# Unread TensorE products, earlier table loads and an earlier second round of routing in the drain of a decoder layer

## The reference, cut to what matters

```python
x = _layernorm(x + attention(x, W_K, W_Q, W_V, W_O))        # causal, 16 heads of 128
x = _layernorm(x + cross_attention(x, ctx_2048, ...))       # 16 heads of 16, 256 image keys
# mixture of experts: E = 8, K = 2, F = 1024
gate_probs = softmax(x @ gate_w + gate_b)
weights, selected = top_k(gate_probs, 2); weights = weights / sum(weights)
h = gelu(einsum('nd,edf->enf', x, w1) + b1)
expert_out = einsum('enf,efd->end', h, w2) + b2
x = _layernorm(x + einsum('ne,end->nd', comb, expert_out))
```

## Time and profile before

| | us |
|---|---|
| median of 3 runs | 613.43 (612.69 to 613.81) |
| the profiled execution, its own time | 612.67 |
| its span | 610.2 |
| PE busy | 548.7 (90%) |
| DVE busy | 366.8 (60%) |
| ACT busy | 309.3 (51%) |
| POOL busy | 169.2 (28%) |

### The profile page before, as it was taken

How to read it: one execution, slowest core, us unless ns; L and a number is a source line. 1 busy time by engine, 2 the same in 40 slices (tenths; PEclk the granted TensorE clock), 3 DMA queues, 4 the chain that set the end, 5 groups by cost and what they waited for, 6 DMA issues and landing times.

```text
span 610.2 us, 12615 instructions
## 1 busy us (share of the span) xinstructions
PE 548.7 (90%) x3875; PEld 478.2 (78%) x3875; DVE 366.8 (60%) x1150; ACT 309.3 (51%) x837; POOL 169.2 (28%) x280
## 2 busy tenths in 40 slices
PE   2899999999999999999987989998769999999930
PEld 2689989898998989899876756655469999999930
DVE  6075565656556565655668657776377456665645
ACT  1365454545545454554554668755553545544523
POOL 5131311213121121301452888041620010000253
PEclk9999999999999999999989789979769999999985
DMA  8740040404104040380000000010211544444124
GB/s 273 254 186 24 31 161 26 180 17 153 54 24 165 22 184 0 138 347 14 1 2 1 1 2 4 2 71 10 87 53 53 179 166 180 173 181 165 61 78 128
DMA packets 18403, 58.75 MB, mean 96 GB/s; under 512 B 3168, under 2 KB 7520, under 8 KB 13760
## 3 DMA queue, kind: packets, MB, share of 16 engines
q1 hardware_dynamic: 14048, 38.00, 17.2%
q10 hardware_dynamic: 1728, 12.58, 5.6%
q0 software_dynamic: 2592, 7.74, 3.6%
HBM read 35.83 MB, written 22.41 MB: 95 GB/s over the span
## 4 chain that ended last, share of the span: by engine, by line
PE 81%; DVE 8%; issue 3%; ACT 2%; DMA 2%; POOL 2%; DVEq 1%; ACTq 0%; POOLq 0%
PE bank L605 13%; PE bank L607 12%; PE bank L606 12%; PE bank L932 8%; PE bank L662 5%; PE bank L644 4%; PE bank L819 4%; PE bank L652 4%; PE bank L835 3%; PE bank L762 2%; PE bank L663 2%; PE bank L643 2%; DVE w_lo L1536 2%; PE bank L869 1%; PE bank L690 1%
## 5 line engine op out<-in xcount | busy, mean ns | idle before, releaser
L1228 ACT ACTIVATE hT<-bank,b 128x128 f32<-128x128 f32 x152 | 53.6, 367 | 63.2 <-PE bank L932 60.1
L932 PE MATMUL bank<-xgT,w 128*128 128x128 f32 x608 | 73.9, 281 | 0.8 <-ACT hT L1228 0.8
L932 PEld LDWEIGHTS bank<-xgT,w 128*128 128x128 f32 x608 | 72.2, 197 | 1.0 <-ACT hT L1228 1.0
L605 PE MATMUL bank<-xT_hi,wqk_hi 128*128 128x512 f32 x128 | 56.8, 444 | 11.0 <-DVE wqk_lo L1283 11.0
L1037 ACT ACTIVATE Pr<-Sm,nmax 128x128 f32<-128x128 f32 x64 | 25.8, 403 | 71.1 <-DVE nmax L1292 71.0
L1292 DVE CUSTOM_DVE_ANT_0 Sm<-bank,mask 128x128 f32<-128x128 f32 (+1 forms) x128 | 40.9, 356 | 34.4 <-PE bank L644 34.3
L1422 DVE TENSOR_REDUCE xnmax<-bank 128x2 f32<-128x512 f32 x64 | 43.7, 687 | 27.3 <-PE bank L798 26.6
L606 PE MATMUL bank<-xT_lo,wqk_hi 128*128 128x512 f32 x128 | 51.1, 399 | 0.0
L607 PE MATMUL bank<-xT_hi,wqk_lo 128*128 128x512 f32 x128 | 51.0, 399 | 0.0
L1128 ACT ACTIVATE xPT<-bank 128x512 f32<-128x512 f32 x64 | 37.7, 597 | 26.2 <-PE bank L819 26.0
L605 PE MATMUL bank<-w_hi,hT_hi 128*128 128x256 f32 x152 | 44.7, 294 | 2.8 <-DVE hT_lo L1549 2.8
(11 more groups left out here) (232 smaller groups left out, 1516.7 us busy)
## 6 DMA issues: line engine op xcount, KB each, us to landing
w<-in_w ACTq DMA_DIRECT2D x12, 1024.0 KB, 6.5
w_raw<-in_w_attn SPq DMA_DIRECT2D x32, 256.0 KB, 3.6
x_slots<-w SPq DMA_DIRECT2D x8, 1024.0 KB, 5.5
y_slots<-w SPq DMA_DIRECT2D x7, 1024.0 KB, 7.4
w<-in_w SPq DMA_DIRECT2D x4, 1024.0 KB, 7.9
y_slots<-ys POOLq DMA_DIRECT2D x19, 128.0 KB, 2.0
xg<-x_slots SPq DMA_DIRECT2D x18, 128.0 KB, 2.1
xT_raw<-in_xT SPq DMA_DIRECT2D x2, 512.0 KB, 5.5
```

Of the source, the lines that this page charges most:

```text
L605: mm(out, lh, rh, start=start, stop=False)
L932: last = mm(ps_h[f % 4][:, 0:P], w1[e % 2][:, c, f * P:(f + 1) * P], xgT[:, c, :], start=c == 0, stop=c == DC - 1)
L1228: A(hT[:, f, :], ps_h[f % 4][:, 0:P], ACT.Gelu_apprx_tanh, bias=b1[:, e, f:f + 1])\
```

## The change

On PE a helper `keep_warm(n, out)` is new: n bf16 products of ones by ones, 128x512, into a bank that is not read before it is started anew. Calls of it stand at six places of the drain: 4 before the third row transposes (`x2t_unit(2)`, in step 69), 3 before the last `z_back` (step 78), 1 before the last output products, 10 before the last row transposes, 2 before the last gate products, 2 behind the transposes of the first static tile. `ffn_tile` is cut in two, `h_products` and `y_products`, and the first three of eight h blocks of the first static tile stand ahead of the last `rank_unit`. Round one moves up: its gate products from step 71 to 70 and ahead of `x_pv`, its ranks from 74 to 72, ACT's evacuation from 70 to 69, DVE's part from 72 and 75 to 71 and 73. On ACT the Sqrt table is loaded behind the last exponential of the items and the Gelu table behind `gate_exp`. On DVE `xgt_evac(2)` stands ahead of the search for the indices, `count_tiles` and `gate_weights` move into the loop over the static tiles, `gate_weights` to the second.

```diff
             def ffn_tile(e, i):
+                h_products(e, i, 0, FC)
+                y_products(e, i)
+            def keep_warm(n, out):
+                for _ in range(n):
+                    mm(out[:, :], ones_bf[:, :], ones_bf[:, :].unsqueeze(1).to_broadcast([P, 4, P]), start=True, stop=True)
...
+                if i == STEPS_X - 3:
+                    keep_warm(3, ps_xt[1])
                 if j >= 13 and (j - 13) % ZUNIT == 0 and j - 13 < ITEMS:
                     z_back((j - 13) // ZUNIT)
+                if i in (61, 70):
+                    gate_unit((61, 70).index(i))
...
+                if i == 69:
+                    pe.wait_ge(s["xmax_ready"], ITEMS)
+                    keep_warm(4, ps_gate)
                 if i in (55, 59, 69):
                     x2t_unit((55, 59, 69).index(i))
-                if i in (61, 71):
-                    gate_unit((61, 71).index(i))
-                if i in (64, 74):
-                    rank_unit((64, 74).index(i))
+                if i in (64, 72):
+                    rank_unit((64, 72).index(i))
+            keep_warm(1, ps_xt[1])
             xo_unit(TT - 2)
             xo_unit(TT - 1)
+            keep_warm(10, ps_xt[1])
             x2t_unit(TT // 2 - 1)
+            keep_warm(2, ps_xt[1])
             gate_unit(2)
             xg_transposes(0)
+            keep_warm(2, ps_xt[1])
+            h_products(0, 0, 0, 3)
             rank_unit(2)
-            for e in range(EARLY):
+            h_products(0, 0, 3, FC)
+            y_products(0, 0)
+            for e in range(1, EARLY):
                 ffn_tile(e, e)
... ACT
-                if i in (56, 60, 70):
-                    x2t_evac((56, 60, 70).index(i))
+                if i in (56, 60, 69):
+                    x2t_evac((56, 60, 69).index(i))
+                if i == ITEMS + LAG:
+                    A(warm[:, :], eps_rms[:, :], ACT.Sqrt)
...
             gate_exp()
+            A(warm[:, :], eps_rms[:, :], ACT.Gelu_apprx_tanh)
... DVE
-                if i == 72:
+                if i == 71:
                     gate_logits(1)
                     gate_index(1)
                     gate_select(1)
-                if i == 75:
+                if i == 73:
                     slots(1)
...
             gate_shift()
+            xgt_evac(2)
             gate_index(2)
             gate_select(2)
-            xgt_evac(2)
             slots(2)
-            count_tiles()
-            gate_weights()
             dve.wait_ge(s["b2_in"], 16)
             for e in range(EARLY):
+                if e == 0:
+                    count_tiles()
                 h_splits(e)
                 xgt_evac(e + 3)
                 if e == 0:
                     w2_low(1)
                 else:
+                    gate_weights()
                     slot_weights()
                 y_add(e, e)
```

More of the change, by code:

```diff
@@ L923, in xg_transposes, with h_products @@
                 last.then_inc(s["xgt_done"], 1)
[L925 to L929, removed]
+            def h_products(e, i, a, z):
+                if a == 0:
+                    pe.wait_ge(s[f"w_in{e % 2}"], 32 * (e // 2 + 1))
+                    pe.wait_ge(s["xgt_ready"], i + 1)
+                for f in range(a, z):
                     pe.wait_ge(s["h_gelu"], i * FC + f + FC - 3)
@@ L934, in ffn_tile, with y_products @@
                     last.then_inc(s["h_done"], 1)
+            def y_products(e, i):
                 xg_transposes(i + 1)
@@ L943, in ffn_tile @@
                 last.then_inc(s["y_done"], 1)
+            def ffn_tile(e, i):
+                h_products(e, i, 0, FC)
[3 more added lines that the diff above has]
+                    mm(out[:, :], ones_bf[:, :], ones_bf[:, :].unsqueeze(1).to_broadcast([P, 4, P]), start=True, stop=True)
             pv(PAIRS - 1, 7)
```

## The result

| | before | changed |
|---|---|---|
| median of 6 executions each | 614.47 us (612.69 to 616.70) | 607.99 us (606.67 to 609.73) |
| ratio | 1 | 0.9895 (95%: 0.9865 to 0.9925) |
| profiled execution, own time | 612.67 us | 606.75 us |
| its span, mean granted clock | 610.2 us, 0.952 | 605.1 us, 0.969 |

The change is faster by 1.05%. In a second comparison, on one chip, the changed kernel took 607.28 us, ratio 0.9876 (0.9850 to 0.9901). The profiled executions differ by 5.9 us, the medians by 6.5 us.

What follows compares the result with a forecast made beforehand. Two chains bound the drain nearly together: PE's products, partly at half clock, and ranks-slots-scatter-load. Tile 2's transposes 4.4 us early, less 0.3 for handovers, gave -4.1: 608.6 profiled, 609.3 beside the median, range 607.9 to 612.3.

Steps and rivals of the forecast that it cites:

- Clock: Drain: unread products in PE's waits hold the granted clock near 1.00 from 428 to 449, where it fell to 0.50.
- The frame: Whole sum: times taken from one profiled execution of before, 612.67 us, span 610.2; median of the runs 613.43.
- Round one: Tiles 4 and 5: with earlier gate products and held clock, the transposes of 438.28 start at 436.15, 2.1 us early.
- Output products to gate: Drain at full clock, Sqrt table loaded early: last row transposes at 441.75 instead of 445.38, gate products done 4.6 us early.
- Unread products: PE's drain waits: each 128x512 bf16 product priced at 0.25 us at full clock, 0.47 at the dear end.
- Rival C: Drain: unread products hold the clock but cost 0.47 us each; slots 1.2 us early, about 612.2 us; chance 0.07.
- Static tile ahead of the ranks: First h blocks before the last ranks: cost 0.35 us on the scatter's chain, gain 1.35 us on PE's.
- Splits of h: First static tile: with gate_weights moved behind, DVE's first split goes from 455.96 to 450.3, second layer starts at 451.25.
- Tile 2: Drain's end: tile 2's transposes at 459.3 instead of 463.69, 4.4 us early, PE waiting some 1.5 us for its rows.
- Rival A: Drain: clock held only in part, still dropping at 428.8; slots 2.4 to 2.8 us early, 610.6 to 611.0; chance 0.24.
- Rival B: Drain: clock falls as before, static tile delays last ranks to 452.1, scatter 1.6 us later; 615.0 us; chance 0.11.
- Table load: ScalarE's Gelu load: 1.28 us in the trace, 2.66 by the skill with its drain; sum -4.1 either way.

Runs made afterwards that it cites:

- ten only: The changed kernel with only the ten unread products before the last row transposes, the other twelve set to zero: 611.69 us, ratio 0.9957.
- late tables: The changed kernel with both early table loads (Sqrt and Gelu, the operations on `warm`) taken out: 607.91 us, ratio 0.9876.

## Why the prediction was right, and where its sizes were off

The forecast was 609.3 us in a range of 607.9 to 612.3; measured were 607.99 and, in the second comparison, 607.28. The first lies just inside the range, by 0.09 us, and the second just outside, so that the time fell in the range is partly luck. The direction and the mechanism hold; the size came out larger, 6.5 us of medians against 4.1. One of these us is that the median of before is 614.47 over six executions and was 613.43 over the three that the forecast was set beside.

- **Clock.** The step was that unread products in the waits keep the clock at 1.00 from 428 on. It holds, and more strongly than told: with the products alone 0.9871, without them 1.000. I had worked out the new order and the tables as equal terms of the sum; none of them shows in a median. In the profiles they are worth 0.6 to 0.8 us of the drain once the clock is held, and nothing was seen of them without it.
- **The frame.** This is the term that was mis-sized. The sum took the drain of before from one profiled execution, 35.31 us with 17.1 at half clock. The second one shows 38.10 with 26.9, and that execution, 614.75 us, lies nearer the medians of before (614.2 to 615.1 of 11 to 17 executions) than the first, 612.67 us. The two profiles of the changed drain show 31.74 and 31.53. So the gain is 3.6 us against the one and 6.4 to 6.6 us against the other; how often before runs either drain is not shown by two profiles. The profiled pair also owes something to chance: 2.4 of the 5.1 us between the first two spans were gained ahead of the first changed instruction (428.38 against 425.98), with 20.5 us at half clock there against 13.7. The twelve profiles without products before the drain begin it anywhere from 424.72 to 429.50 us, with the change or without.
- **Round one**: forecast 2.1 us up to `z_back`, measured 1.8 (A 9.90 to 8.09). The two waits for ACT, 0.62 and 0.63 us, that PE meets around the last products with V were not in my list.
- **Output products to gate**: forecast 1.5 and 0.1 us from `z_back` on, measured 1.34 and 0.03 (B, C). The Sqrt load was priced at 1.2 at the new pace and is worth 0.94. The eight output products were to take 2.06 us at full clock and take 1.99.
- **Unread products**: 0.25 us each were taken between 0 and 0.47; ten take 2.32 us, so 0.23 each. Rival C is out. Started at half clock they can cost, as the ten in the kernel with ten only show.
- **Static tile ahead of the ranks**: priced at 0.35 us on the scatter's chain; undoing it gives 0.46 (D 3.69 to 3.23). DVE's copy ahead of the search costs another 0.33, which I had told of without a price. Both are losses of the change on the chain that binds tile 2 at full clock.
- **Splits of h**: forecast second layer 5.9 us early, measured 5.07 (28.78 to 23.71 from the third row transposes). With gate_weights put back it is 1.7 us later, and PE's wait in front of it 3.60 instead of 1.89 us.
- **Tile 2**: forecast 4.4 us early, measured 3.57 (35.31 to 31.74). The wait for its load, forecast at 1 to 1.5 us, is not in the first profile of the changed kernel: the clock fell behind the wait for the splits, as was allowed for, and PE used the time up with the second layer at half clock (4.14 us). It is there in the second profile of the changed kernel, at full clock, and in five experiments, 0.67 to 1.16 us. In these six profiles E is 12.54 to 12.73 us although D runs from 2.90 to 5.83, which speaks for that chain. With SyncE's reading of bounds ahead of the wait the load is issued 1.45 us sooner behind the last scatter, and PE no longer waits for it.
- **Rival A** (only part of the clock held) is in kind what the kernel with ten only does: 611.69 us, where 610.6 to 611.0 was worked out for a shorter fall (3.4 us at half clock and not 17). **Rival B** (the static tile delays the last ranks at half clock) is what the kernel without products shows: ranks 2.7 us behind the start of the h blocks, tile 2 at 39.30 us. Its condition did not arise in the changed kernel.
- **Table load.** The Trainium skill, ScalarE: Activation LUTs, section What ACT_TABLE_LOAD costs, adds a drain of about 1.38 us to a load. It was not seen here either: the operation on `warm` starts 0.01 us behind the load (443.33 + 1.28, 444.62), and in the kernel with late tables the load starts 0.01 us behind the copies of w2 (436.35 + 3.22, 439.58).

After tile 2 the changed kernel gave back some 0.9 us in its first profile (147.4 against 146.5 us to the end). Most tiles take 6.66 to 6.75 or 7.5 us in every kernel; one of the changed kernel's took 7.98. Eight of the thirteen profiles, both of before among them, have one or two such tiles, of 7.68 to 8.21 us, so this is no sign of the change. Its cause is open.

## What to carry to other kernels

Where TensorE waits again and again for 1 to 3 us, look at the granted clock behind each wait before trimming the work in it: here 22 products that nobody reads, in waits that were there anyway, gave in the median what the whole change gave, and ten of them in one wait a third of it. They should end before what they stand in front of is ready, at half clock too, and they do not hold the clock every time. When the clock varies between executions, profile the kernel more than once before building a sum on one drain; and once the clock is held, ask again which chain binds, since here work moved in front of the ranks lengthened the one that did (D 3.69 us, 2.90 with both moves undone).

## What the runs showed of the hardware

- Bf16 products of 128x512 start every 0.22 us at full clock: ten take 2.32 us, one alone 0.38 us, so nine more cost 1.94.
- Once fallen, the clock can stay at 0.50 for 17 to 27 us although PE is busy for most of the time (14.74 of 17.10 us in the second profile of before; 20.94 of 27.3 in the kernel without products).
- The order without the products gave two groups of executions 5 us apart, with mean granted clocks of 0.96 and 0.945, in one and the same program.
